# A Perceiver block on one core: its feed-forward on 22 tiles of the inner dimension instead of 24, its loads issued during the self-attention, and the cross-attention's outputs scaled once per head

## The reference

```python
q = (x @ Wq + bq).reshape(1, B * N, H, hd)            # H 16, hd 64
kv = (cond @ Wkv + bkv).reshape(1, -1, 2, H, hd)      # 8192 rows
q = _fq_sym(q, axis=-1); k = _fq_sym(k, axis=-1); v = _fq_sym(v, axis=2)
attn = jax.nn.softmax(einsum('bhqd,bhkd->bhqk', q, k), axis=-1)
attn = _fq_unsigned(attn, axis=-1)
out = einsum('bhqk,bhkd->bhqd', attn, v);  return out @ Wp + bp
...
I = 2816                                              # inner size, 22 tiles of 128
w_gu = _dequant_fp4(gate_up_packed, gate_up_scales, 128)
w_down = _dequant_fp4(down_packed, down_scales, 128)
h = silu(gate) * up                                   # gate, up = x @ w_gu.T
y = einsum('bsi,hi->bsh', h, w_down);  return y / rms
...
x = x + xattn(layernorm(x), ctx);  x = x + attn(layernorm(x));  x = x + ffn(layernorm(x))
```

## Time and profile before

| What | us |
|---|---|
| Median of 3 runs (2914.75 to 2917.15) | 2915.75 |
| The profiled execution's own time | 2918.6 |
| Its span, first to last instruction | 2916.8 |
| PE busy, of the span | 2616.7 (90%) |
| DVE busy | 1856.0 (64%) |
| ACT busy | 1042.6 (36%) |
| POOL busy | 551.9 (19%) |

### The profile page before, as it was taken

One profiled execution on the slowest core, in us unless ns is written; L12 is line 12 of the kernel. 1 busy time (PEld: TensorE's weight loads), 2 busy tenths in 40 slices (PEclk: granted clock), 3 DMA queues, 4 the chain that ended last, 5 costly groups with the idle time before them and its releaser, 6 DMA issues. The chain is left out here.

```text
span 2916.8 us, 42666 instructions
## 1 busy us (share of the span) xinstructions
PE 2616.7 (90%) x16824; PEld 1331.0 (46%) x16824; DVE 1856.0 (64%) x2875; ACT 1042.6 (36%) x930; POOL 551.9 (19%) x208
## 2 busy tenths in 40 slices
PE   6999999999999999999777777777769999499998
PEld 3444444444444444444344444444444476244443
DVE  5855555555555555555699999999934343466663
ACT  3111111111111111111389999999942132211100
POOL 0400000000000000000364654654510811011100
PEclk9999999999999999999899999999979977699999
DMA  6243444344434443343478888888762200300000
GB/s 239 71 102 85 109 115 105 82 108 115 102 88 105 115 108 88 99 115 100 131 174 209 183 193 211 180 197 203 159 212 87 87 1 1 61 15 15 8 1 29
DMA packets 557201, 321.44 MB, mean 110 GB/s; under 512 B 401952, under 2 KB 533280, under 8 KB 552352
## 3 DMA queue, kind: packets, MB, share of 16 engines
q1 hardware_dynamic: 557088, 319.78, 43.2%
HBM read 149.82 MB, written 69.21 MB: 75 GB/s over the span
## 5 line engine op out<-in xcount | busy, mean ns | idle before, releaser
L498 PE MATMUL kv_acc<-kv_whi,kv_xthi 128*128 128x512 f16 x2048 | 778.1, 380 | 5.7 <-DVE kv_xtlo L554 5.7
L498 PE MATMUL kv_acc<-kv_wlo,kv_xthi 128*128 128x512 f16 x2048 | 778.0, 380 | 0.0
L498 PE MATMUL kv_acc<-kv_whi,kv_xtlo 128*128 128x512 f16 x2048 | 777.9, 380 | 0.0
L950 DVE TENSOR_SCALAR_CACHE_REDUCE at_sc<-at_score 128x1024 f32<-128x1024 f32 x512 | 612.3, 1219 | 16.9 <-PE at_score L832 12.4
L1053 ACT ACTIVATE at_sc<-at_sc,at_bias,at_qs 128x4096 uint16<-128x4096 f32 x128 | 484.8, 3790 | 1.1 <-DVE at_bias L962 1.1
L541 ACT ACTIVATE kv_parts<-kv_key 128x1024 f16<-128x1024 f32 x64 | 67.6, 1057 | 863.3 <-DVE kv_key L579 863.3
L498 PEld LDWEIGHTS kv_acc<-kv_whi,kv_xthi 128*128 128x128 f16 x2048 | 200.6, 98 | 248.2 <-DVE kv_xtlo L554 6.2
L498 PEld LDWEIGHTS kv_acc<-kv_whi,kv_xtlo 128*128 128x128 f16 x2048 | 200.6, 98 | 242.4 <-issue 1.4
L498 PEld LDWEIGHTS kv_acc<-kv_wlo,kv_xthi 128*128 128x128 f16 x2048 | 200.6, 98 | 242.0 <-issue 1.1
L560 DVE SCALAR_TENSOR_TENSOR kv_key<-kv_acc,kv_bias 128x512 f32<-128x512 f32 x128 | 88.5, 691 | 339.1 <-PE kv_acc L498 339.1
L847 PE MATMUL at_turn<-ident,at_sc 128*128 128x128 f16 x2048 | 151.3, 224 | 121.7 <-DVE at_probt L968 91.3
(11 more groups left out here) (189 smaller groups left out, 3359.6 us busy)
## 6 DMA issues: line engine op xcount, KB each, us to landing
kv_rows<-in_ctx SPq DMA_DIRECT2D x64, 512.0 KB, 8.1
keys_turned<-kv_kt SPq DMA_DIRECT2D x32, 1024.0 KB, 5.2
values<-kv_val SPq DMA_DIRECT2D x32, 1024.0 KB, 9.4
at_v_raw<-values SPq DMA_DIRECT2D x16, 2048.0 KB, 8.6
at_kt<-keys_turned SPq DMA_DIRECT2D x32, 512.0 KB, 5.2
x<-keys_turned SPq DMA_DIRECT2D x31, 512.0 KB, 5.1
wq_stage<-in_wkv SPq DMA_DIRECT2D x4, 2048.0 KB, 7.8
x<-in_x SPq DMA_DIRECT2D x2, 2048.0 KB, 8.3
```

The lines of the kernel that those rows point to most:

```text
L498: last = nc.tensor.matmul(acc[c][:], a[s][:, k, :], b[:, c, k, :], start=(k == 0 and q == 0), stop=(k == KD - 1 and q == 2))
L950: nc.vector.tensor_scalar(sc[n % 2][:, c * SC:(c + 1) * SC], score[pos % 2][:], 1.0, None, ALU.mult, ALU.max, accum_out=part_max[n % 2][:, ...
```

## The change

Four things are changed. The feed-forward works on the 22 tiles that the inner dimension has; the third group of words of the down projection holds only 6 of its 8 codes, laid out by bytes, and `Weights.make` uses four shorter multiplications there with three rows of scales. Words, scales and the bias row of the output projection are loaded in a block of `attend_causal`, into memory that the transposed queries and keys have left, and the last weight panel (number 9) is split between groups of that attention. The projection "po", the layer norm and the feed-forward are one block, `project_and_feed_forward`, in which PE goes through the projection tile by tile, and DVE normalises each tile when it is there. In the cross-attention the four tiles of a head keep their sums in one PSUM bank; DVE divides all four at once, in the second slot of the next head, and the value's scale is multiplied by POOL when it moves the output to `o`.

```diff
+H_TILES = INNER // P
-NCH_UP, NCH = NB * WORD // 2, NB * WORD // 2 + 2 * NB
+NCH_UP, NCH = H_TILES // 2, H_TILES // 2 + 2 * NB
...
             def move_out(i, j):
                 head = 2 * i + j
-                pool.wait_ge(o_taken, TAKEN0 + i * SLOTS + T * (j + 1))
-                nc.gpsimd.tensor_copy(o[:, :, bass.ds(head * HD, HD)], o_pair[j][:]).then_inc(o_moved, 1)
+                pool.wait_ge(o_taken, TAKEN0 + head + 1)
+                nc.gpsimd.tensor_tensor(o[:, :, bass.ds(head * HD, HD)], o_pair[j][:],
+                                        vs_pair[j][:].unsqueeze(1).to_broadcast((P, T, HD)), ALU.mult).then_inc(o_moved, 1)
...
-                    pe.wait_ge(o_taken, TAKEN0 + g + 1 - 2)
+                        pe.wait_ge(o_taken, TAKEN0 + head + 1 - 2)
...
+            def output(head, j):
+                dve.wait_ge(inv_step, INV0 + 2 * head + 2)
+                dve.wait_ge(dma_summed, DSUM0 + T * (head + 1))
+                dve.wait_ge(o_moved, MOVED0 + head + 1 - 2)
+                nc.vector.tensor_tensor(o_pair[j][:], outp[j], inv[j][:].unsqueeze(2).to_broadcast((P, T, HD)),
+                                        ALU.mult).then_inc(o_taken, 1)
...
+                        done = None if n % T > 1 or first and n < 2 else 2 * i - 1 + n // T
+                        j = (n // T + 1) % 2
+                        if done is not None and n % T == 0 and c == 5:
+                            total_sum(done, j)
+                        if done is not None and n % T == 0 and c == 6:
+                            inverse(done, j)
+                        if done is not None and n % T == 1 and c == 0:
+                            output(done, j)
...
+        @block.sync
+        def _(sp):
+            sp.dma_start(*row).then_inc(feed.row_loaded, 16)
+            feed.load(sp, 0)
+            feed.load_scales(sp)
+            feed.load(sp, 1)
+            feed.load(sp, 2)
...
             masks(0)
             for g in range(G):
+                if g == G // 2:
+                    panels.low(dve, split)
...
                 turned_out(g)
+                if g == G // 4:
+                    panels.high(act, split)
...
+            if self.short(c):
+                four = [v.rearrange("p (k e) n -> p k e n", e=2) for v in (dst, codes)]
+                nc.vector.tensor_tensor(four[0][:, 0:2], four[1][:, 0:2],
+                                        part[:, 0:3:2, :].unsqueeze(1).to_broadcast((P, 2, 2, HALF)),
+                                        ALU.mult).then_inc(self.ready, 1)
+                nc.vector.tensor_tensor(four[0][:, 2:4, 0, :], four[1][:, 2:4, 0, :],
+                                        part[:, 1:2, :].to_broadcast((P, 2, HALF)), ALU.mult).then_inc(self.ready, 1)
...
+            for n in range(len(units)):
+                turn_o(n)
+            pe.wait_ge(panels.lo_ready, first + 2)
+            for t in range(T):
+                for n in range(2):
+                    products(t, n)
+                if t:
+                    turn_x(2 * t - 2)
+                    turn_x(2 * t - 1)
+            turn_x(2 * T - 2)
+            turn_x(2 * T - 1)
...
+                tiles = [k for k in range(WORD) if b < NB - 1 or NIBBLE[k] < LAST]
...
+            for n in range(len(units)):
+                low_o(n)
             make(0)
+            dve.wait_ge(row_added, 1)
+            for t in range(T):
+                take_x(t, 0)
+                take_x(t, 1)
+                normalise(t)
+                if t:
+                    low_x(2 * t - 2)
+                    low_x(2 * t - 1)
+            low_x(2 * T - 2)
+            low_x(2 * T - 1)
             make(1)
...
+            for n in range(len(units)):
+                high_o(n)
+            act.wait_ge(feed.raw_loaded, 16 * GROUPS)
             nc.scalar.activation(scale[:, 0, :], scale[:, 0, :], ACT.Copy, scale=SC_SCALE).then_inc(scaled, 1)
+            nc.scalar.activation(scale[:, 1:NSC, :], scale[:, 1:NSC, :], ACT.Copy, scale=SC_SCALE).then_inc(scaled, 1)
+            for t in range(T):
+                root(t)
+                if t:
+                    high_x(2 * t - 2)
+                    high_x(2 * t - 1)
```

More of the change, by code:

```diff
@@ L989, in body @@
                     g = i * SLOTS + n
-                    before = not (first and n == 0)
                     for c in range(CH):
@@ L994, in body @@
                             copy(i, ahead, pos)
[L995 to L1002, removed]
-                            if before:
-                                total_sum(g - 1, (n - 1) % SLOTS)
-                            if biased:
-                                make_bias(i * SLOTS + ahead, ahead)
-                        if c == 6 and before:
-                            inverse(g - 1, (n - 1) % SLOTS)
+                        if c == 1 and not (first and n == 0):
+                            turned_out(i * SLOTS + n - 1)
+                        done = None if n % T > 1 or first and n < 2 else 2 * i - 1 + n // T
[6 more added lines that the diff above has]
+                            output(done, j)
+                        if c == 5 and not (last and ahead >= SLOTS):
+                            find_max(i * SLOTS + ahead, ahead)
+                            make_bias(i * SLOTS + ahead, ahead)
             dve.wait_ge(vs_turned, 1)
@@ L1098, in rotate, with attend_causal @@
     return n + 4 * T
-def attend_causal(chip, y_q, y_k, y_v, mask, o, ident32):
+def attend_causal(chip, y_q, y_k, y_v, mask, o, ident32, q_t, panels, split, feed, row):
     nc = chip.nc
@@ L1280, in make, with scales_of, short, made @@
+    def scales_of(self, c):
+        half, b = divmod(c - NCH_UP, NB)
+        first = c if c < NCH_UP else NCH_UP + half * (NB - 1 + SLOTS_LAST) + b
+        return first, SLOTS_LAST if self.short(c) else 1
+    def short(self, c):
+        return c >= NCH_UP and (c - NCH_UP) % NB == NB - 1
+    def made(self, c):
+        return sum(4 if self.short(n) else 2 for n in range(c))
     def make(self, dve, c, words, freed, count):
         nc, at = self.nc, self.STEPS * c
-        scale = self.scale[:, c, :]
+        first, slots = self.scales_of(c)
+        scale = self.scale[:, first:first + slots, :]
+        coarse, fine = self.coarse[:, 0:slots, :], self.fine[:, 0:slots, :]
@@ L1301, in make, with project_and_feed_forward @@
             dve.wait_ge(freed, count)
[L1302 to L1304 removed]
+        for part, dst in ((coarse, self.hi[c % 2]), (fine, self.lo[c % 2])):
+            if self.short(c):
[5 more added lines that the diff above has]
+                                        part[:, 1:2, :].to_broadcast((P, 2, HALF)), ALU.mult).then_inc(self.ready, 1)
+            else:
+                nc.vector.tensor_tensor(dst, codes, part.to_broadcast((P, WORD, HALF)), ALU.mult)\
+                    .then_inc(self.ready, 1)
     def wait(self, pe, c):
[L1307 to L1310 removed]
+        pe.wait_ge(self.ready, self.made(c + 1))
+def project_and_feed_forward(chip, panels, first, feed, room, o, x, row, ident32, out_d):
     nc = chip.nc
@@ L1604 @@
+            attend_causal(chip, y_q, y_k, y_v, mask, o, ident32, q_t, panels, 9, feed,
+                          (bias[:, 0, :], flat_bcast(a["bo"], D)))
+            project_and_feed_forward(chip, panels, 8, feed, room, o, x, bias[:, 0, :], ident32, out_d)
 def kernel(x, ctx_2048, L0_xattn_Wq, L0_xattn_bq, L0_xattn_Wkv, L0_xattn_bkv, L0_xattn_Wp, L0_xattn_bp,
```

361 lines of the change are left out of this document (225 added, 136 removed).

## The result

The changed kernel takes 2849.89 us (median of 4 runs, 2849.09 to 2850.45), beside 2915.32 for the kernel before (4 runs): a ratio of 0.9771, 95% interval 0.9759 to 0.9784, so 65.4 us less. The forecast was 2837 with 2827 to 2850. The profiled execution took 2849.09 us with a span of 2847.3, beside 2918.6 and 2916.8: 69.5 us of span to explain, where the forecast had 78.5.

A forecast was written before the change was run, and what follows sets the result against it. It took PE to bound the feed-forward, with waits before the first gate product, and an ACT-DVE-PE loop the cross-attention. Terms -31.1 - 38.2 + 2.8 - 12 = -78.5 gave 2840.1 us profiled, 2837 as median, range 2827 to 2850.

The forecast's parts named there:

- Fewer tiles: Feed-forward: fewer matmuls save 20.7 us in gate and up and 10.4 in both down halves, -31.1 in sum.
- The way from "po" to the first gate product: Merged block: from the first transpose of `o` to the first gate product 56.9 us against 95.1, so -38.2.
- Rival D: Merged block: DVE's unpacking ahead of the takes delays tile 0's rows, PE waits 3 to 9 us; 2843; chance 0.13.
- B: Cross-attention: ACT is the pace, and its whole 0.39 us wait goes in nearly each slot; 2825 us; chance 0.07.
- Panel 9: Self-attention: splitting this weight panel between groups adds 1.0 us on ACT and 1.7 on DVE, together +2.8.
- Cross-attention: Three of each head's four slots lose 0.30 us, one gains 0.14; -0.76 per head, -12 for 16 heads.
- The output lies in this loop for 0.30 us: Cross-attention: DVE's output is part of the ACT, DVE, PE loop that sets the 10.80 us slot.
- rival A: Cross-attention gives nothing: PE's queue or transposing DMAs set the fourth group, the output filled a hole; 2849; chance 0.12.
- The clock: First gate products: PE's cold start at the lower clock stays, so no gain; -2.5 us if the clock holds.
- rival C: First gate products: the clock holds through the short idleness before them; 2834.5 us; chance 0.18.
- The sum: Whole launch: -78.5 us, profiled execution 2918.6 to 2840.1; median 2.85 lower, so 2837; chance 0.47.

The follow-up runs named there:

- plain_unpack_late: plain_after with the unpacking of chunk 0 moved back behind the last low half on DVE; 2856.15 us, beside 2844.03 for plain_after.
- plain_late_loads: plain_after with the loads of bias row, first words and scales issued at the start of the merged block; 2866.96 us, beside 2844.03.
- plain_split_late: plain_after with the split of weight panel 9 moved from the self-attention to the start of the merged block; 2853.76 us, beside 2844.03.
- turns_apart_before: The kernel before, with the second group of transposes in a cross-attention slot put behind the scores; 2911.31 us, ratio 0.9976.
- plain_undo_headwise: plain_after with the cross-attention of the kernel before (sums, inverses and outputs for every slot); 2844.80 us, beside 2844.03 for plain_after.
- plain_turns_apart: plain_after with the second group of eight transposes put behind the next chunk's scores on PE; 2834.23 us, beside 2844.03 for plain_after.
- plain_warm: plain_after with 17 unread matmuls in PE's waits around the last tile's transposes of x; 2840.89 us, beside 2844.03 for plain_after.
- plain_before: The kernel before, with plain transfers in place of turning ones for keys and half of the probabilities (attention computes something else); 2912.72 us.
- plain_after: The changed kernel, with plain transfers in place of turning ones for keys and half of the probabilities (attention computes something else); 2844.03 us.

## Why the prediction was right and where it was wrong

*Fewer tiles*, -31.1: -20.3 in gate and up and -5.2 in each half of down, 30.7 together. Right. The missing 0.4 is the clock: at 0.2158 us a matmul, its slow stretch cost 2.5 us before and 2.9 now.

*The way from "po" to the first gate product*, 56.9: 57.0. The last 8.0 behind the projection: 7.9. Rival D, a late queue of DVE, didn't happen: no wait of PE stands between the products. Nor did B: ACT still waits 0.40 us for the fourth group. plain_unpack_late and plain_late_loads show two parts of the gain by themselves, 10.3 us for unpacking beside the products and 20.5 for the early loads (77.4 us of way in place of 56.9). These are 30.8 of the 38.1 measured. The rest, norm and transposes tile by tile, was not taken back by itself, and no run took back both parts at once, so how they overlap stays open.

*Panel 9*, +2.8: +2.5. Measured by the starts of the reciprocals, a group takes 4.73 us and the two with the split 5.52 and 6.21, so 0.8 and 1.5 longer where 1.0 and 1.7 were forecast. The other 0.25 stand ahead of the first reciprocal, in plain_split_late and plain_late_loads too, so they are neither the split's nor the loads'.

*Cross-attention*, -12: the step that failed is "The output lies in this loop for 0.30 us". There were 0.30 us between its start and the next copy, but the copy also waited for scores. With scores that came earlier it started 0.20 behind the output's start (turns_apart_before), so in the kernel before they were late by 0.10, and they did not move with the output. Taking the output away left the copy where it was, and 0.3 us was gained in the slots, some 1 at most in the launch (plain_undo_headwise) in place of 12. This is rival A, which had 0.12; its reason ("the output only filled a hole") was right, and its guess of what sets the slot only in part: PE's queue it is, but by the transposes between exponential and scores, and not by the fourth group or the transfers. plain_turns_apart shows it: with half of these transposes behind the scores, the slots are the predicted 10.50 us. The argument against A, that the third group waits for DVE's copy, was true and no answer, as that copy had a second thing to wait for. The rows that I had read carry no wait at the copy of 1901.27, since the output's row (0.28 us) covers it.

*The clock*: it started cold, as the sum had it. plain_warm prices rival C at 2.7 us in gate and up, beside 2.5. Why "ps" ran fast behind its transposes in the kernel before is not settled. There are 32 of them in a row, and the mean granted clock was 0.54 during them and 1.00 behind them:

```profile
2217.00:2223.50 6.50, 6.35 (x33) 6.34 (x34) 5.85 (x10) 3.82 (x7) 0.00 (x0) 0.54 0.01 3
2223.50:2227.00 3.50, 3.50 (x19) 1.61 (x17) 1.68 (x3) 3.50 (x3) 0.00 (x0) 1.00 0.00 0
```

Here 8 stand between idle stretches of 3.65 and 1.41 us. So the prediction's reason, that short transposes would not release the clock, is not borne out by "ps", though its result came true.

*The sum*: with 1 in place of 12 the terms give 67.5 for the span, beside 69.5 measured. The remaining 2 lie ahead of the self-attention, within the scatter named above; from the first exponential to the last the two kernels differ by only 0.6 us, so they are not a gain of the headwise output. Against the forecast the profiled execution is 9.0 us longer (2849.09 to 2840.1). The median missed by 12.9, since I had set it 2.85 below the profiled time, as in the kernel before, and here it lies 0.8 above. So the time stands at the upper end of the range for two reasons: 9 us of terms, and 3.65 of one execution taken for the rule. The range held it by 0.1 us, and only because it had been drawn to take in rival A; the forecast itself, with its 0.47, did not come true in the cross-attention.

## What to carry to other kernels

An instruction that stands on a loop without an idle gap may still be free: before it is priced at its length, look up when the next instruction's other inputs arrive, and take the smaller of the two. Where a queue holds work that nobody waits for yet (here eight transposes) ahead of work that closes the loop (the scores), swapping the two can be worth more than removing an instruction: 6.6 us against 0.3 to 1 here, each by itself. Moving loads and unpacking one stage earlier was counted to 0.1 us by the chain here (57.0 beside 56.9), with each engine's queue in the new place written out with its times; where the issue and the norm were left out (plain_late_loads), the count was 4 to 9 us for a wait of 18.5.

## What was not expected of the hardware

- The eight transfers that spread the scales took 18.19 us from the last issue to landing in the earlier trace rows, and 24.78 in plain_late_loads. Both stand behind the first words; in the second each transfer is 336 KB in place of 288 KB, and the bias row stands ahead. If the time went with the bytes, it would be 21.2 us, an estimate from these rows; what the rest is stays open.
- The cost of a wait on PE is more than its length. Behind 8.65 us of waiting 96 products took 3.1 us more than warm, at a granted clock of 0.50 in their first 4.8 us (plain_split_late). Behind 18.5 us of it, eight transposes took 1.1 more (1.97 to 0.89) and the 48 products behind them 0.9 (11.26 to 10.36; plain_late_loads). In the changed kernel itself two short waits, 3.65 and 1.41 us with eight transposes between them, cost 1.1 in the transposes and 2.9 in the products. So a wait in which the clock fell cost 2 to 4 us beyond its length in these runs.
- 17 matmuls that nobody reads, in waits of 3.65 and 1.41 us, held the clock at 1.00 and delayed nothing (plain_warm).
- Transfers that turn and that end last in no ordinary slot still cost 3 to 6 us in all beside plain ones (plain_before, plain_after), a part of it by holding SP's queue ahead of another load.
